# Matmuls into an unread PSUM bank at nine places of TensorE's program

## The reference

```python
xn = _layernorm(x)
deg_out, deg_in = segment_sum(ones, src), segment_sum(ones, dst)      # at least 1
agg = segment_sum((xn * rsqrt(deg_out))[src], dst)                    # gather and sum over edges
g = relu((agg * rsqrt(deg_in)) @ W + b);  gnn = g / norm(g)
q, k, v = split(xn @ w_qkv.T)                                         # 8 heads of 64
k, v = instance_norm(k), instance_norm(v)
mix = (q @ (k.T @ v) / N) @ w_out.T + b_out                           # per head
x = x + gnn + mix
x = x + ffn(_layernorm(x))   # 8 experts, top 1, 1024 hidden, capacity 977 rows each
```

## Time and profile before

| | before |
|---|---|
| time, median of 3 runs | 1342.82 us (1341.68 to 1342.93) |
| the profiled execution, its time | 1343.66 us |
| its span, first to last instruction | 1342.4 us |
| mean granted TensorE clock | 0.977 |
| PE busy, 13487 matmuls | 1242.2 us, 93% |
| DVE busy | 1118.1 us, 83% |
| POOL busy | 921.7 us, 69% |
| ACT busy | 861.3 us, 64% |

### The profile page before, as it was taken

How to read it: one execution, slowest core, us unless ns; L and a number is a source line. 1 busy time by engine, 2 the same in 40 slices (tenths; PEclk the granted TensorE clock), 3 DMA queues, 4 the chain that set the end, 5 groups by cost and what they waited for, 6 DMA issues and landing times. The chain is left out here.

```text
span 1342.4 us, 37027 instructions
## 1 busy us (share of the span) xinstructions
PE 1242.2 (93%) x13487; PEld 1042.9 (78%) x13489; DVE 1118.1 (83%) x2065; ACT 861.3 (64%) x2018; POOL 921.7 (69%) x706
## 2 busy tenths in 40 slices
PE   4799999986989999999999999999988999899986
PEld 4466666643878999998899998999874979888986
DVE  7899999988989888788888988888964777768776
ACT  4588888776545666666666666666654666584654
POOL 6457774224278887887788888888845587767574
PEclk9799999996999999999999999999999999999999
DMA  9212111003945654556444555544534343442220
GB/s 303 67 41 57 54 46 33 30 25 135 248 93 118 117 103 105 101 102 134 92 96 94 124 98 115 121 93 96 114 91 144 136 148 95 130 131 84 89 71 27
DMA packets 99519, 137.49 MB, mean 102 GB/s; under 512 B 16102, under 2 KB 76030, under 8 KB 99345
## 3 DMA queue, kind: packets, MB, share of 16 engines
q0 software_dynamic: 49040, 68.09, 26.3%
q1 hardware_dynamic: 50320, 67.33, 15.1%
HBM read 96.93 MB, written 47.45 MB: 108 GB/s over the span
## 5 line engine op out<-in xcount | busy, mean ns | idle before, releaser
L1821 PE MATMUL bank<-reg_b,reg_a 128*128 128x256 f16 x4116 | 550.6, 273 | 2.0 <-ACT reg_a L1385 1.9
L1078 POOL DMA_INDIRECT reg_a<-h_rows,reg_w x229 | 426.0, 1860 | 70.8 <-issue 69.5
L1385 ACT ACTIVATE reg_a<-bank 128x392 f16<-128x392 f32 x672 | 322.2, 497 | 213.2 <-PE bank L1813 205.7
L2143 DVE TENSOR_TENSOR reg_c<-iota_v,reg_c 128x2048 f16<-128x2048 f16 (+1 forms) x270 | 353.3, 1325 | 63.0 <-PE bank L1813 57.8
L1821 PEld LDWEIGHTS bank<-reg_b,reg_a 128*128 128x128 f16 x4116 | 367.3, 97 | 38.8 <-issue 2.7
L1813 PE MATMUL bank<-reg_a,reg_c 128*128 128x98 f16 x2688 | 224.9, 209 | 11.0 <-ACTq L1504 4.5
L1813 PEld LDWEIGHTS bank<-reg_a,reg_c 128*128 128x128 f16 x2688 | 185.2, 99 | 26.7 <-issue 13.0
L2143 DVE TENSOR_TENSOR reg_a<-iota_h,reg_c 128x1568 f16<-128x1568 f16 x168 | 162.6, 968 | 0.0
L2099 PE MATMUL bank<-w_hi,hid_hi 128*128 128x256 f32 (+1 forms) x368 | 107.4, 292 | 11.6 <-DVE w_lo L2887 6.3
L2101 PE MATMUL bank<-w_hi,hid_lo 128*128 128x256 f32 (+1 forms) x368 | 104.8, 285 | 0.0
L2100 PE MATMUL bank<-w_lo,hid_hi 128*128 128x256 f32 (+1 forms) x368 | 104.7, 285 | 0.0
(11 more groups left out here) (408 smaller groups left out, 2407.0 us busy)
## 6 DMA issues: line engine op xcount, KB each, us to landing
reg_b<-in_L_ffn_w SPq DMA_DIRECT2D x16, 1024.0 KB, 5.0
h_rows<-reg_b POOLq DMA_DIRECT2D x14, 896.0 KB, 10.2
tok_rows<-reg_e SPq DMA_DIRECT2D x24, 512.0 KB
x_t<-in_x SPq DMA_DIRECT2D x24, 256.0 KB
xnT_t<-xnT_rows SPq DMA_DIRECT2D x24, 256.0 KB
out<-reg_e SPq DMA_DIRECT2D x24, 256.0 KB
reg_a<-h_rows,reg_w POOLq DMA_INDIRECT x245
xnT_rows<-xnT_t SPq DMA_DIRECT2D x13, 256.0 KB, 2.0
```

Source lines behind the costliest of these rows:

```text
L1078: ins = g.indirect_dma_start(out=acc[i % 2][r][k], out_offset=None, in_=h_rows, in_offset=at, compute_op=ALU.add)
L1385: return a.activation(AT[k].rearrange("p h (w t) -> p h w t", w=2)[:, :, :, s * GROUP:(s + 1) * GROUP], tile_ps[bk][:, 0:GROUP * 2 * NB].r ...
L1821: ins = t_.matmul(agg_ps[k][:, 0:D], AT[k][:, h, :], h_all[:, half, h, :], start=(first and h + half == 0), stop=(last and h == NB - 1 and ...
L2143: return v_.tensor_tensor(out.rearrange("p t (v u) -> p t v u", u=2), iota.rearrange("p (v u) -> p v u", u=2).unsqueeze(1).to_broadcast(sh ...
```

## The change

`idle(n)` issues n matmuls of 128 columns (the constant `ones16` by the 128 x 128 identity, both fp16) into 128 columns of bank 0, or of bank 5 in one place. Nobody reads the result. It is called with 32, 10, 12, 24, 36, 20, 72, 64 and 56, 326 matmuls in all, each once in an execution. Four waits come with it, so that bank 0 is free: for `row_set`, and for `hw_out` at 1, NB - 2 and NB.

```diff
+    idle_ps = bank[0][:, 0:P]
...
+        def idle(n, ps=idle_ps):
+            for _ in range(n):
+                t_.matmul(ps, ones16[:, :], ident16[:, :], start=True, stop=True)
...
                 hist(s, s % HBUF)
                 if s == 1:
+                    pe.wait_ge(row_set, 1)
+                    idle(32)
                     column_norms()
...
                 if s == 2:
+                    idle(10)
                     tiles_T(0)
+                    idle(12)
                 if s == 3:
                     pe.wait_ge(consts, 21)
                     tiles_less(0, 0)
+                    idle(24)
...
             if fixed(q, NQ):
+                pe.wait_ge(hw_out, NB - 2)
+                idle(72)
                 pe.wait_ge(key_out, 1)
...
         def hw_rows(q, k, m):
             if fixed(q, 0) and m == 0:
+                idle(36)
                 pe.wait_ge(unit_lo, 3)
...
                         hist(s, s % HBUF)
+                        if s == HFIRST:
+                            pe.wait_ge(hw_out, 1)
+                            idle(20)
...
                 if (q, n) == (NQ - 1, 0):
                     block_keys(0, 0)
+                    idle(64, bank[5][:, 0:P])
                     pe.wait_ge(more_set, 1)
...
         def last_sums():
+            pe.wait_ge(hw_out, NB)
+            idle(56)
             kv_sums(NQ, 0)
```

## The result

The changed kernel takes 1346.02 us (median of 12 runs, 1340.8 to 1348.95), the kernel before beside it 1342.07 us (12 runs, 1341.28 to 1344.07). The ratio is 1.0026, 95% interval 1.0017 to 1.0035: slower by 0.26%, or 3.5 us. The profiled execution took 1346.37 us, its span 1345.2. Its mean clock is higher than before, 0.986 against 0.977, and it is slower all the same.

A forecast was written before the change was run, and what follows sets the result against it. DVE and ACT mostly set the pace, TensorE only from its first dense sum at 342.84 us. Terms -2.9 - 0.3 + 4.4 = +1.2 us gave 1344.9 against the profiled execution, 1344.0 against the median; range 1339.0 to 1348.0.

The forecast's parts named there:

- Price of an idle matmul: One idle matmul of 128 columns on TensorE takes 56 ns at full clock, 0.11 us at half.
- Part 1: First pairs (32, 10, 12, 24, 36, 20): faster second kv_rows lets DVE go on earlier, 2.9 us gained, bounds 0 and 4.4.
- The second fall: First pairs, third kv_rows: behind the unfilled gap of 1.95 us the clock falls as before, for 3.4 us.
- One step: First pairs: a hole of over 2 us stays behind the 36, so the clock still drops once at 41 us.
- Part 2: Last pair and lone tile (64, 72): 0.3 us gained, bounds 0 and 1.7, or -1.6 if the 72 run at half clock.
- one sign: Lone tile, profile after: the clock is still half at 312 us less the shift.
- the other: Lone tile, profile after: DVE's wait at L2218 is still over 1.5 us.
- Part 3: Ahead of the last sums: the 56 start only behind TensorE's branch, mostly at half clock; DVE 4.4 us late, bounds 1.7 and 5.2.
- Its faster matmuls between 326 and 335 give nothing back: Behind the last sums: TensorE's faster matmuls bring no gain, since they wait for DVE's one-hots.
- the later falls of the clock: Behind the branches at 375 us and between the stages: they move with the shift and may add or save 1 us.
- the 56 are hidden: Rival, ahead of the last sums: the 56 fill the gap of 4.87 us and cost nothing, 1339.6 us; chance 0.25.
- the clock isn't held: Rival: idle matmuls don't bring full clock back, first pairs gain nothing, the 56 cost 5.2 us; 1348.3 us, chance 0.2.

The follow-up runs named there:

- best: First eight calls, plus 20 idle matmuls ahead of strip 7, 44 ahead of the builds at s = 12, 60 at the sparse path, none behind the branch: ratio 0.9972 to before.
- no56: The changed kernel without its last call (the 56 and their wait): ratio 0.9987 to the kernel before.
- no56b: The changed kernel without its last call (the 56 and their wait), run again: ratio 0.9991 to the kernel before.
- part1: The kernel before with the first six calls alone (32, 10, 12, 24, 36, 20): ratio 0.9975 to the kernel before.
- fill12: The changed kernel with 44 more idle matmuls ahead of the builds at s = 12 of block 0: ratio 0.9982 to the kernel before.
- only56pad: The kernel before with the 56 in the taken branch and 112 idle matmuls in the one not taken: ratio 1.0034 to the kernel before.
- ahead56: The kernel before with the 56 and their wait ahead of the branch instead of behind it: ratio 1.006 to the kernel before.
- only56: The kernel before with the last call (the 56 and their wait) alone: ratio 1.0081 to the kernel before.
- only56b: The kernel before with the last call (the 56 and their wait) alone, run again: ratio 1.0101 to the kernel before.
- dead56: The kernel before with the 56 only in the branch not taken, so no added matmul executes: ratio 1.0029 to the kernel before.

## Why the prediction was right, and where its sum was off

Forecast were 1344.0 us and +1.2 on the kernel before; measured were 1346.02 and a ratio that means +3.5 us. The range of 1339.0 to 1348.0 holds it. The mechanisms that the prediction named were there: the gain in the first pairs, and the 56 in series behind the branch. But its sum was near in part by luck. Its three terms were forecast as -2.9 - 0.3 + 4.4 = +1.2 us; in the profiles they came to -2.7 - 1.4 + 3.1 = -1.0, and the changed kernel does reach the memset 1.05 us earlier than before (326.65 against 327.70). With these three alone it would have been faster. What took it above the kernel before came with falls of the clock behind the memset, which the sum didn't have: +2.6 us from the memset to the dense sum and +1.3 later on, which makes +2.8 between the spans.

**Price of an idle matmul.** 56 ns was taken. The 64 took 3.75 us with the tail of the last (0.2 us), 55 ns each; the 81 ns that the prediction names beside its own are not borne out here.

**Part 1, 2.9 us.** Measured were 2.7 us (62.93 to 60.21), by the steps forecast: the second kv_rows is 2.76 us long, and the waits are 0.38 and 1.72 us for 0.35 and 1.6. The second fall stayed, because of the gap left open, which best shows by filling it. One step was wrong without effect: the clock did not fall at 41 us in the changed kernel.

**Part 2, 0.3 us.** Measured were 1.4 us: 4.2 at the memset less the 2.7 of part 1. The prediction had the 72 start right behind kv_rows and end long before the transposes. They stand behind the wait for xn_t, so they started at 304.27, ran in part at half clock (0.50 in the windows of 304 to 306 us) and ended some 0.6 us after the transposes were due, with the clock up. hw_rows and the sums then took 0.82 and 0.69 us. So one sign failed, the clock still half at 312 us less the shift (it was 1.00), and the other held, a wait of over 1.5 us (1.72). The term was within its bounds, 0 to 1.7.

**Part 3, 4.4 us.** The place was right: behind the branch, in series, and DVE waits for it. Without the 56 and without a break the wait is 0 (no56, no56b, part1, best), with the 56 it is 3.11 to 3.37 us wherever no break adds to it. The 4.4 was too much, nearly all of it in one term: the clock came back at 324 us, and the 56 took 4.66 us from their start to that of the last sums, and not 5.8.

**What the sum lacked.** "Its faster matmuls between 326 and 335 give nothing back" was true and not enough: they take. They made a gap of 1.22 us into one of 3.55, the clock fell in it, and the second product on the path to the dense sum lost 2.5 us. fill12 shows it: 2.6 us back with this gap filled. And the later falls of the clock, for which 1 us to either side was left, cost 1.3 us in the profile of the first chip: 1.0 us behind 375 and 1.4 behind 814 us, less 1.1 that came back between and behind them. Why they fell otherwise than before was not tested.

**The rivals.** That the 56 are hidden is excluded by no56 and only56pad, and but for a small part by ahead56. That the clock isn't held is excluded by part1. What is left open: the changed kernel's runs on the first chip spread over 8.2 us, those of before over 2.8. That the second product takes 3.68 or 5.37 us with the same code may be a part of it; no runs but the profiled ones were traced. In device time, the price of the 56 is shown only where they stand alone (only56, only56b, only56pad); for the changed kernel it is shown in the traces.

The rule of "Runtime: NRT & Kernel Launch" of the Trainium skill, section "Instruction fetch mechanics", is that a taken branch to code that is not held forces a fetch before execution goes on. The traces agree: TensorE stands for 4.75 to 5.23 us behind the branch in every version but ahead56 (in four of them the profile names DVE's v, which was there 0.2 to 1.0 us earlier). The same section of the Trainium skill calls the cost of crossing from one block of code to the next mostly hidden. The 7.81 us of dead56 would be such a crossing that wasn't hidden; that they are one is not shown, only that this wait comes with the place of the code.

## What to carry to other kernels

Matmuls that hold the clock paid here only where they fitted into a wait and another engine waited for TensorE's matmuls behind it: of the nine calls the first six gained 2.7 us, and the last, behind a branch, cost 3.1 us. Of the waits that the profile puts down to "issue", the one of 4.9 us behind the branch took nothing in, while the one of 2.67 us at 23 us, with no branch of the program ahead of it, took all of the 32. So the word "issue" alone doesn't tell whether a gap can be filled. The faster TensorE made a longer wait further on: look there for the next fall of the clock, before you count the gain.

## What the runs showed of the hardware that was not expected

Code that never runs can cost time. 112 instructions more in the branch not taken moved the code of the taken one, and TensorE broke off for 7.81 us behind 12 matmuls of it (dead56). With another 112 that break was gone; one of 2.45 us stood further on, where it did no harm (only56pad). So of two kernels that differ in the code of a branch, one may have 7 us of waiting that the other hasn't: look at the waits for issue before comparing them.

The mean clock was no guide to the time: it is 0.986 after against 0.977 before, and the kernel is 3.5 us slower.
